# Second cross-attention: three of each quad's four head biases added by GpSimd in SBUF, one by VectorE; late exponentials in another order on ScalarE

## The reference, cut to what matters

```python
def _L1_xattn_ref(query, key, value, attn_mask, key_padding_mask, Wq, bq, Wk, bk, Wv, bv, Wo, bo):
    B, L, S, E, H = (4, 256, 256, 128, 16)
    DH = E // H
    SCALING = DH ** (-0.5)
    q = (query @ Wq.T + bq) * SCALING
    k = key @ Wk.T + bk
    v = value @ Wv.T + bv
    q, k, v = (_split_heads(q), _split_heads(k), _split_heads(v))
    scores = jnp.einsum('bhld,bhsd->bhls', q, k)
    scores = scores + attn_mask[None, None, :, :]
    scores = jnp.where(key_padding_mask[:, None, None, :], -jnp.inf, scores)
    probs = jax.nn.softmax(scores.astype(jnp.float32), axis=-1).astype(scores.dtype)
    attn = jnp.einsum('bhls,bhsd->bhld', probs, v)
    attn = attn.transpose(0, 2, 1, 3).reshape(query.shape[0], query.shape[1], E)
    return attn @ Wo.T + bo
```

## Time and profile before

| | |
|---|---|
| time, median of 3 runs | 592.15 us (591.96 to 592.64) |
| the profiled execution's own time | 594.53 us |
| its span, first to last instruction | 592.6 us |
| TensorE busy / VectorE / ScalarE / GpSimd | 520.1 / 455.6 / 280.5 / 169.3 us |
| mean granted clock of TensorE | 0.945 |
| the stage of the second cross-attention with loose quads | about 475 to 549 us |
| VectorE's bias adds in it (L1082), copies (L996), late exponentials (L1002), GpSimd's adds (L2156) | 0.69, 0.60, 0.63, 1.27 us each; 28 copies, 28 late exponentials, 28 GpSimd adds |

### The profile page before, as it was taken

How to read it: one execution, slowest core, us unless ns; L and a number is a source line. 1 busy time by engine, 2 the same in 40 slices (tenths; PEclk the granted TensorE clock), 3 DMA queues, 4 the chain that set the end, 5 groups by cost and what they waited for, 6 DMA issues and landing times.

```text
span 592.6 us, 9188 instructions
## 1 busy us (share of the span) xinstructions
PE 520.1 (88%) x3218; PEld 303.0 (51%) x3227; DVE 455.6 (77%) x1185; ACT 280.5 (47%) x489; POOL 169.3 (29%) x130
## 2 busy tenths in 40 slices
PE   7798999999999999999999954575659999999866
PEld 5344666666666666566666510121224555666423
DVE  6689866775773366676455789999998689999997
ACT  4540455555542244244233344655540377777465
POOL 8623000000000000020000015899994145554221
PEclk9899899999998899999999995778888999999989
DMA  5100340000100000100000000000000100000001
GB/s 135 29 13 0 118 132 2 2 1 3 45 1 0 1 1 1 37 5 2 0 1 0 2 0 0 0 1 1 0 0 0 46 2 2 3 2 1 2 0 37
DMA packets 10769, 9.27 MB, mean 16 GB/s; under 512 B 2050, under 2 KB 9540, under 8 KB 10724
## 3 DMA queue, kind: packets, MB, share of 16 engines
q1 hardware_dynamic: 10724, 8.69, 5.1%
HBM read 6.98 MB, written 0.52 MB: 13 GB/s over the span
## 4 chain that ended last, share of the span: by engine, by line
PE 65%; DVE 17%; POOL 9%; issue 4%; ACT 4%; POOLq 0%; DVEq 0%; ACTq 0%
PE PS L1219 19%; PE PS L758 10%; PE PS L1245 10%; PE PS L820 5%; PE PS L803 5%; POOL E L1746 4%; POOL KSA L1738 3%; DVE PS L1788 2%; PE PS L778 2%; PE PS L471 2%; PE PS L1648 1%; PE PS L830 1%; PE PS L734 1%; POOL OT L1731 1%; DVE VA L1801 1%
## 5 line engine op out<-in xcount | busy, mean ns | idle before, releaser
L1219 PE MATMUL PS<-XNT,KSA 128*128 128x512 f32 x256 | 120.5, 605 | 0.0
L803 PE MATMUL PS<-QM,KP 32*128 32x256 f32 x512 | 91.9, 398 | 1.2 <-ACT E L991 0.8
L1227 ACT ACTIVATE E<-PS 128x512 f32<-128x512 f32 x64 | 38.1, 597 | 108.6 <-PE PS L1219 108.4
L1233 DVE TENSOR_TENSOR E<-E,PS 128x512 f32<-128x512 f32 x64 | 43.9, 687 | 57.5 <-ACT E L1227 56.1
L758 PE MATMUL PS<-KP,QP 32*128 32x256 f32 x512 | 78.1, 401 | 0.2 <-ACT QP L969 0.2
L991 ACT ACTIVATE E<-PS 128x512 f32<-128x512 f32 x100 | 56.1, 595 | 35.0 <-PE PS L803 24.3
L1245 PEld LDWEIGHTS PS<-KSA,E 128*128 128x128 f32 x512 | 63.6, 196 | 17.1 <-issue 15.9
L1219 PEld LDWEIGHTS PS<-XNT,KSA 128*128 128x128 f32 x256 | 45.5, 192 | 42.0 <-issue 41.8
L1245 PE MATMUL PS<-KSA,E 128*128 128x128 f32 x512 | 63.6, 278 | 0.4 <-DVE XN L1454 0.4
L803 PEld LDWEIGHTS PS<-QM,KP 32*128 32x128 f32 x512 | 60.5, 184 | 6.2 <-issue 4.8
L308 PE MATMUL PS<-KSA,select 128*128 128x512 bf16 x62 | 25.1, 495 | 40.9 <-ACT KSA L1685 29.1
(11 more groups left out here) (287 smaller groups left out, 909.1 us busy)
## 6 DMA issues: line engine op xcount, KB each, us to landing
KSA<-in_w SPq DMA_DIRECT2D x2, 1024.0 KB, 6.8
X<-in_x SPq DMA_DIRECT2D x2, 256.0 KB, 3.3
SCR<-in_ctxT SPq DMA_DIRECT2D x1, 512.0 KB, 5.5
KP<-OT SPq DMA_DIRECT2D x16, 32.0 KB
SCR<-in_fside SPq DMA_DIRECT2D x1, 512.0 KB, 4.6
KP<-QM SPq DMA_DIRECT2D x16, 32.0 KB
out_x<-X SPq DMA_DIRECT2D x8, 64.0 KB, 1.5
wx<-in_w_x SPq DMA_DIRECT2D x1, 384.0 KB, 6.6
```

The costliest lines, as they stand in the source:

```text
L803: ins = pe.matmul(o[:, kt * S:(kt + 1) * S], KP[rows(i), g, t:t + P], QM[rows(i), g, b * S:(b + 1) * S], start=True, stop=True, skip_group ...
L1219: ins = pe.matmul(bank(2 * (g % 3) + o), w[:, e, c * P:(c + 1) * P], XNT[:, tokens_of(p)], start=True, stop=True)
L1227: act.activation(E6[:, 4 + g % 2, :], bank(2 * (g % 3)), ACT.Silu).then_inc(sig("silu"), 1)
L1233: dve.tensor_tensor(E6[:, g % 4, :], E6[:, 4 + g % 2, :], bank(2 * (g % 3) + 1), ALU.mult)\
```

## The change

Three things. Item j = 2 of the loose quads goes the second way: `LOOSE` is (0, 2, 3), and VectorE adds the bias of j = 1 alone. `loose` finds six places in place of four: the four of before and two in `SCR[:, 3, :]`. The late exponentials stand elsewhere in ScalarE's queue: (m-1,2) behind the copy of (m,0), (m-1,3) behind the exponential of (m,1), and (m,0) behind the copy of (m,2). The counts on which weighing and late exponentials wait follow.

```diff
-            return L == 1 and (m >= LOOSE_QUADS or j in (1, 2))
+            return L == 1 and (m >= LOOSE_QUADS or j == 1)
...
-        LOOSE = (0, 3)
+        LOOSE = (0, 2, 3)
...
         def loose(m, j):
-            k = 2 * (m % 2) + LOOSE.index(j)
-            return VAf[:, 2 * T + k * HALF:2 * T + (k + 1) * HALF]
+            k = len(LOOSE) * (m % 2) + LOOSE.index(j)
+            home = VAf[:, 2 * T:4 * T] if k < 4 else SCR[:, 3, :]
+            return home[:, k % 4 * HALF:(k % 4 + 1) * HALF]
...
                 if L == 1:
-                    pe.wait_ge(sig("late_exps"), 2 * min(m + 1, LOOSE_QUADS))
+                    pe.wait_ge(sig("late_exps"), len(LOOSE) * min(m + 1, LOOSE_QUADS))
...
-                act.wait_ge(sig("loose_biased"), 2 * m + LOOSE.index(j) + 1)
+                act.wait_ge(sig("loose_biased"), len(LOOSE) * m + LOOSE.index(j) + 1)
...
-                    if j == 0 and k > LAG and pool_bias(L, k - LAG - 1, 3):
+                    if j == 0 and k > LAG and pool_bias(L, k - LAG - 1, 2):
+                        late_exps(k - LAG - 1, 2)
+                    if j == 1 and k > LAG and pool_bias(L, k - LAG - 1, 3):
                         late_exps(k - LAG - 1, 3)
-                    if j == 1 and pool_bias(L, k - LAG, 0):
+                    if j == 2 and pool_bias(L, k - LAG, 0):
                         late_exps(k - LAG, 0)
```

More of the change, by code:

```diff
@@ L680, in vector_bias @@
         def vector_bias(L, m, j):
-            return L == 1 and (m >= LOOSE_QUADS or j in (1, 2))
+            return L == 1 and (m >= LOOSE_QUADS or j == 1)
         def biased_by(m, j):
-            return 2 * m + j if m < LOOSE_QUADS else 2 * LOOSE_QUADS + HG * (m - LOOSE_QUADS) + j + 1
-        LOOSE = (0, 3)
+            return m + 1 if m < LOOSE_QUADS else LOOSE_QUADS + HG * (m - LOOSE_QUADS) + j + 1
+        LOOSE = (0, 2, 3)
         def pool_bias(L, m, j):
```

## The result

| | before | after |
|---|---|---|
| time, median | 592.15 us (591.96 to 592.95, 5 runs) | 617.03 us (613.05 to 618.09, 5 runs) |
| ratio to before | | 1.0403 (95% interval 1.0381 to 1.0424) |
| profiled execution, its span | 594.53, 592.6 us | 613.05, 611.3 us |
| copies, GpSimd adds, late exponentials | 28 each | 42 each |

The change costs 4.0%, or 24.9 us between the medians. I had forecast slower, 607.0 us, in 602.0 to 613.0: the sign and the mechanism came out, the size did not. The five runs after spread over 5.0 us and the five before over 1.0; but 17 runs of the kernel before, taken beside the experiments, spread over 5.9 (591.27 to 597.13), so the spread by itself is no sign of the change.

A forecast was written before the change was run, and what follows sets the result against it. It took a loop through VectorE, ScalarE and TensorE (4.78 us a round), with VectorE full in later rounds, as the bound. Round 3 +1.03, rounds 4 to 15 +13.10, round 16 +0.78: +14.9 on 592.15 gives 607.0, range 602.0 to 613.0.

The forecast's parts named there:

- The old loop: Second cross-attention: second pair, maximum, bias of (m,2), exponential, release of (m,1); 4.78 us a round, to go with the change.
- The new chain: Late exponential (m-1,3) waits behind (m,1)'s exponential: weighing 4.58 us behind first pair, round 5.59 without output part.
- output parts on the path: TensorE's output work between weighing and next first pair, hidden before, now adds 0.37 to 0.64 us: rounds 5.96 to 6.23.
- round 3: First round with the new wait: weighing moves from 482.83 to 483.86, +1.03 us.
- the twelve rounds: Rounds 4 to 15: 12 x 5.59 plus 4.38 of output parts, 71.46 against 58.36, +13.10 us.
- round 16: No maxima, four ScalarE activations ahead of the weighing: 4.23 us behind first pair against 3.45 before, +0.78.
- The price of 0.14: From the late exponential's end to TensorE's weighing, 0.14 us, between 0.05 and 0.25; its ends move the sum -1.3 to +1.5.
- rival 2: TensorE idle before each weighing lowers its granted clock; two such rounds 612 us, half of them 625; chance 9 in 100.
- the price of a fall: At the lower clock TensorE's parts on the new path double: 1.15 + 1.01 + 0.5 = 2.7 us a round.
- the two that I had allowed in the range: The range to 613.0 held the clock's fall for one or two rounds; two such rounds give 612 us.
- Rival 1: Late exponential (m-1,3) does not hold the weighing; TensorE's own work sets rounds of some 4.2, 584 us; chance 3 in 100.
- Rival 3: GpSimd's adds delay VectorE's maxima and bias, 1.26 us a round, 16.4 on top: 623 us; chance 2 in 100.

The follow-up runs named there:

- e3_fill: The changed kernel with ten unused matmuls ahead of each weighing of a loose quad, to keep TensorE busy; 608.12 us, ratio 1.0256.
- e2_order_only: The kernel before with only the late exponential of (m-1,3) moved behind the exponential of (m,1), two heads staying with VectorE; 617.06 us, ratio 1.0428.
- e1_two_ahead: The changed kernel with the late exponential of (m-1,3) again ahead of the exponential of (m,1), behind that of (m-1,2); 590.45 us, ratio 0.9961.
- e5_bias_ahead: The changed kernel with VectorE's bias of (m,1) ahead of the maximum (k,1) in loose quads; 601.46 us, ratio 1.0123.
- e4_last_head: The changed kernel with VectorE's one head at j = 3, GpSimd's at 0, 1, 2, late exponentials placed to suit; 590.95 us, ratio 0.9960.
- e7_two_ahead_tail: e1_two_ahead with the late exponentials (13,2) and (13,3) first in ScalarE's queue in round 16; 587.64 us, ratio 0.9908.

## Why the prediction was right in the mechanism and wrong in the size

**The old loop** went as said: the shifted scores (m,1) no longer wait, and the second pair starts 1.46 behind the first.

**The new chain** was right term by term: 4.54 measured against 4.58, 5.59 and 5.54 against 5.59 for a round, output parts on the path (5.95 to 6.28 measured, 5.96 to 6.23 forecast). With the clock held at 1.00, `e3_fill` measures it whole. Its parts: round 3, 481.76 - 477.21 = 4.55 in the changed kernel against 3.55 before, 1.00; the twelve rounds 71.29 - 58.36 = 12.93; round 16, 5.80 - 5.04 = 0.76. Sum 14.7, forecast 14.9; and the run itself is at 608.1, forecast 607.0. The price of 0.14 for the release of the weighing was 0.10 (492.79 to 492.89). The first pair of round 3, from which the 4.55 counts:

```profile
477.21 0.48 PE L759 MATMUL PS<-KP,QP 32*128 32x256 f32 x1
```

**The step that failed is the clock**, rival 2, which I gave 9 in 100 and left out of the sum. Two things were wrong in it. I argued that a TensorE busy three quarters of the time speaks against a fall, and looked at one fall only, behind sparse work. The trace of before had others, and one stretch of it contradicts the argument: here TensorE is busy 20.00 of 20 us, no row of it has a wait, and the granted clock is 0.83 all the same. Below it the same stretch of the changed kernel, in a part of the program that the change does not touch:

```profile
180.00:200.00 20.00, 20.00 (x78) 12.72 (x78) 6.30 (x20) 3.26 (x6) 0.00 (x0) 0.83 0.00 1
```
```profile
180.00:200.00 20.00, 20.00 (x94) 13.04 (x93) 7.41 (x24) 5.25 (x9) 0.00 (x0) 1.00 0.00 1
```

So a high busy share did not keep the clock up even before. The changed stage is busy 7.3 to 8.6 of 10 us and the clock fell in it four times in the profiled execution, where the sum had no fall. And I put the price of a fall too high, 2.7 a round, as if weighing, output part and first pair all ran slow. Measured, a round with a slow weighing is 1.4 to 1.6 longer (7.17 against 5.56, the mean of 5.59 and 5.54; 7.58 against 6.17; 7.77 against 6.28): the clock was back within the first pair. So there were more falls than the two that I had allowed in the range, each cheaper than I had priced it.

The profiled execution adds up. Chain 14.7; the falls in the rounds up to 15, (557.59 - 481.76) - 71.29 = 4.54; the one in round 16, (570.97 - 563.39) - (552.27 - 546.23) = 1.54; and this execution's stage began 2.07 earlier (477.21 against 479.28). That lies ahead of everything that the change touches, and it is the clock again: the pair of exponentials at 163.62 of the kernel before stands at 164.87 in the changed one, 1.25 later, but the one at 201.44 stands at 199.35, 2.09 earlier. In between lies the stretch of 180 to 200 us above, with its low clock in the kernel before alone. The sum is 14.69 + 4.54 + 1.54 - 2.07 = 18.70, and the spans differ by 18.7. The weighings of rounds 16 and 18 in the kernel before, for the 6.04:

```profile
546.23 1.07 PE L820 MATMUL PS<-E,VX 128*32 128x256 f32 x16
...
552.27 1.07 PE L820 MATMUL PS<-E,VX 128*32 128x256 f32 x16
```

The changed kernel's median lies 8.9 above `e3_fill`, its profiled execution only 4.8. That the other four executions (615.72 to 618.09) had more falls in the stage is likely but not shown: only one execution of a kernel has a trace. `e2_order_only`, with the same chain, has six slow weighings in an execution of 615.37; five of them, in rounds 6 to 14, cost (560.21 - 481.28) - 71.29 = 7.64, 1.5 each. But a part of the difference can also lie outside the stage, as the 2.07 did, and the mean granted clocks of the five executions do not order them: 0.938 at 613.05, 0.942 at 615.72, 0.939 at 617.03, 0.936 at 618.04 and 618.09.

**Rival 1** (the late exponential does not hold the weighing) was not so, but `e1_two_ahead` makes it so by hand, and its price was off as well: I had counted a round of 4.2 and 584 us; it is 4.62 on average over rounds 3 to 15 (480.68 to 536.14), and 590.5, or 587.6 with round 16 mended. The term is the second pair, 1.66 (501.24 to 502.90) and not 1.15, since its banks come free late.

**Rival 3** (GpSimd and VectorE in each other's way) did not show: the bias add took 0.69 at 490.90, inside GpSimd's adds of 487.77 to 491.52, and `e1_two_ahead`, with GpSimd busy 8.1 of 10 us, is faster than before. The warning of the Trainium skill, "Perfetto Trace Analysis", section "Optimizing Scalar/DVE Operations", is not borne out for these operands.

The row of these adds in the changed kernel:

```profile
487.77 3.75 POOL L2159 TENSOR_TENSOR VA<-VA,KSA 128x512 f32<-128x512 f32 x3 [1.80 <-ACT VA L997]
```

**What stays open** is why the clock falls in some rounds and not in others of nearly the same shape; no run here settles that. In `e2_order_only` all six falls are in even rounds, from 6 to 16; in the changed kernel one of the four is in an odd one, round 7.

## What to carry to other kernels

Look first at what a moved instruction stands behind in its own engine's queue, and which engine waits for it: one late exponential placed behind one that waits for another engine closed a loop through a whole round and cost 24.9 us, where the best order of the same offload gave 5.7 (587.64 against 593.33). Price a new wait of TensorE twice, once for its length and once for the clock; where the wait can't be removed, unused matmuls in it gave back 8.9 of 24.9 us here. And before relieving a full engine, work out what the next one's round is with all its waits for buffers, since that is all that can be won.

## What the runs showed of the hardware

I had not expected TensorE's granted clock to fall in a stage in which it is busy 7.3 to 8.6 of 10 us. With waits of 1.33 to 1.38 us in rounds of 5.5 to 6.3 it fell at three of the twelve weighings of rounds 4 to 15 (five of twelve in `e2_order_only`), with waits of 0.64 to 0.69 us in rounds of 4.9 to 5.6 at none of these twelve, and with the waits filled at none. One longer wait was enough in round 16: it fell there after 1.63 us (the changed kernel and `e5_bias_ahead`), 1.23 (`e4_last_head`) and 1.15 (`e1_two_ahead`), and not after 0.50 (`e7_two_ahead_tail`). Yet the profile does not show idle time ahead of every fall: in the kernel before it was 0.83 from 180 to 200 us, with TensorE busy 20.00 of 20 us by the profile, whose ends are modelled. A fall in the changed stage made a weighing 1.94 us in place of 1.07 and its round 1.4 to 1.6 us longer.
